# Causal attention in a vision transformer tower: element-major head stacks loaded in six transfers, class values by one bf16 product, tile loops written out

## The chip, the cores and the metric

The kernel runs on one core of one Trainium2 chip. The metric is the device time of one execution in microseconds (us), the median of three runs. Engine names follow the profile: PE is TensorE (matrix products), PEld its weight loads, DVE is VectorE, ACT is ScalarE, POOL is GpSimd, SP is SyncE, which here does nothing but issue DMA transfers.

## What is computed

The reference is a small tower on 8 images of 512 patches with 256 features, to which one class token per image is added in front. After a token projection four residual steps follow: a causal attention block with a feed-forward part, an FFN with blockwise 4-bit rounding, a state space block with a scan, and a last block with softmax attention plus a mixture of experts. The change is about the causal attention, with 16 heads of 16 features:

```python
def _attention(x, wq, bq, wk, bk, wv, bv, wo, bo):
    q = (x @ wq.T + bq).reshape(b, s, NH, D).transpose(0, 2, 1, 3)
    k = (x @ wk.T + bk).reshape(b, s, NH, D).transpose(0, 2, 1, 3)
    v = (x @ wv.T + bv).reshape(b, s, NH, D).transpose(0, 2, 1, 3)
    scores = jnp.einsum('bhqd,bhkd->bhqk', q, k) / jnp.sqrt(jnp.float32(D))
    causal = jnp.tril(jnp.ones((s, s), jnp.float32))
    att = jax.nn.relu(scores) * causal
    att = att / (jnp.sum(att, axis=-1, keepdims=True) + 1e-09)
    ctx = jnp.einsum('bhqk,bhkd->bhqd', att, v)
```

The weights are relu(score), not an exponential. The class token is key 0 and every query may look at it, so each patch query has one weight for the class key beside its 512 causal ones; the class query itself sees only its own key. The last block has the same 16 heads with a full softmax.

## The kernel before

Tokens lie in 33 tiles of 128: tile 0 holds the 8 class tokens, the other 32 are four tiles for each of 8 images ("batches"). The residual streams env.x, env.h and env.o stay in SBUF. The kernel is a row of passes, each with one program for each engine and semaphores between them; each pass frees its semaphores in `Area.clear` (L116) and closes with a barrier of all engines. The order of work in an engine's program is written out by hand. The passes, with their stretch of the trace in us: constants and tokens (0 to 180), `pass_qkv` (180 to 314), `pass_causal` (315 to 553), `pass_mlp` (554 to 860), `pass_fp4` (866 to 1188), `pass_ssm_in` (1190 to 1315), `pass_scan` (to 1383), `pass_moe` (to 1797), `pass_attend` (to 2276).

**Tile loops.** The generator `tiles` (L57) gives an engine its first three or five tiles written out, then a hardware loop of two tiles per turn, then a written-out tail. In the loop the values of waits and the addresses are computed in registers. `known(s)` is the tile number where it is a Python number and 9 in the loop.

**pass_qkv.** Per tile PE transposes the normalised tile (L495), forms q and k with 8 products (L505), v with 2 (L512), and 2 products of q with the class key, the scores against key 0 (L523, `class_scores`). DVE forms the statistics (L412, L415) and the normalised tile z (L421); POOL adds epsilon (`qkv_ve`, L406) and takes the power -1/2 (`qkv_rs`, L408). q and k in fp32 (`qkf`) are split in three bf16 parts each, whose sum is the fp32 number: ACT casts part 0 (L566), DVE subtracts it (`rest`, L622) and casts part 1 (L624), POOL subtracts again to part 2 (L588, `third`, three tiles behind the statistics). ACT takes relu of the class scores (`cls_s`, L572). SP writes per tile the parts (`qk_parts`, L463), v (L466) and the class scores (`cls_w`, L459) to scratch DRAM.

**pass_causal.** A product of two fp32 numbers is formed as six products of bf16 parts, all in one pass of PE: for one head of 16 elements the stack `qs` has 16 x 6 = 96 rows, with part PQ = (0,0,0,1,1,2) of q in the six rows of an element, and `ks` the part PK = (0,1,2,0,1,0) of k. `load_half` (L663) fills the stacks of 8 heads for one batch by 12 transfers of 16 rows each (L671), and loads the values (L672) and the class scores (L674). The 8 batches have 4 groups of 4 heads, in all 32 groups. A group has four key tiles: `scores` (L743, four heads, 512, 384, 256 and 128 query columns), relu and mask by ACT (L802, two heads, with POOL's mask of the diagonal block, L833) and by DVE (L863, the other two), then `values` (L757, fp32 weights by v, with a column of ones that sums them). Before a group's values `class_value` (L748) adds the class key's part: an fp32 product of `vbd`, 16 rows with the class value of each head in its own block, and `cls_w`, 16 rows with the class scores of the batch. `turn` (L769) transposes a finished group and DVE divides it.

At the start of the pass SP loads the class row of v, the constants `own`, `pick` and `causal` (L710 to L713), and then both halves of batch 0. PE forms `c8` (L728), spreads the class values over the heads (L732), DVE multiplies them by `own` into `vbd`, and only then do the scores begin. Later batches are loaded in a loop, each half when the values of the batch before it are done.

The stack part of `pass_attend` (`Heads.load`) fills its stacks in the same way, from the parts that `pass_moe` writes.

## Time and profile before

| | us |
|---|---|
| median of 3 runs | 2281.74 (2280.27 to 2282.27) |
| the profiled execution, its own time | 2278.18 |
| span of the trace in that execution | 2276.4 |
| PE busy in the span | 2098.8 (92%) |
| DVE / ACT / POOL busy | 1594.1 / 907.1 / 737.6 |

The span goes from the first to the last instruction in the trace; the execution's own time is 1.8 us longer. The median of the runs lies 3.6 us over the profiled execution. In the rows further down, a line of a timeline has start, duration, engine, line of the kernel, operation, output and inputs, shape, count, and in square brackets the time that the engine sat idle before it and what it waited for. A line of the view by windows has the stretch, its length, then busy time and instruction count of PE, PEld, DVE, ACT and POOL, the granted clock of PE (1.00 is full), the busy share of the DMA engines and GB/s. `SPq` is the issue of a DMA by SP.

### The profile page before, as it was taken

What the parts mean: (1) busy time and instruction counts of PE and PEld (TensorE: products, weight loads), DVE (VectorE), ACT (ScalarE), POOL (GpSimd) and SP (SyncE); (2) the same over time, 40 slices, a digit from 0 to 9 for tenths busy, and PEclk for the clock granted to TensorE, in tenths of its full rate; (3) what the DMA queues carried; (4) which work ended last, traced back from release to release, by engine and by line L of the source; (5) the groups of instructions that cost most, each with busy time, mean ns of one, the idle gap of its engine ahead of it and who ended that gap; (6) DMA issues with size and microseconds to landing.
All of it is one profiled execution on the core that took longest, in us unless ns stands there. A gap on an engine that the chain in (4) does not pass through costs nothing. (4 is left out here: it accounts for less than half of the span.)

```text
span 2276.4 us, 41030 instructions
## 1 busy us (share of the span) xinstructions
PE 2098.8 (92%) x11587; PEld 1337.9 (59%) x11587; DVE 1594.1 (70%) x4366; ACT 907.1 (40%) x2124; POOL 737.6 (32%) x1350
## 2 busy tenths in 40 slices
PE   7998969998999997999988958999999999999998
PEld 6886833333888885666663316888888523333332
DVE  3336846665677776888866856776777788888882
ACT  1114635553221223444433431222222157777777
POOL 3554525554333332333422101111111423333222
PEclk9998979998999999999998968999999779999999
DMA  4323665443000000000001010212214302232210
GB/s 135 114 90 86 152 181 144 138 133 108 1 0 0 0 0 14 1 0 0 0 24 37 9 31 20 48 37 47 46 38 125 89 10 76 81 95 78 76 44 20
DMA packets 215394, 132.43 MB, mean 58 GB/s; under 512 B 116675, under 2 KB 204309, under 8 KB 215317
## 3 DMA queue, kind: packets, MB, share of 16 engines
q1 hardware_dynamic: 215316, 131.50, 21.4%
q8 instruction: 36, 0.59, 0.1%
q14 instruction: 42, 0.34, 0.0%
HBM read 89.81 MB, written 41.25 MB: 58 GB/s over the span
## 5 line engine op out<-in xcount | busy, mean ns | idle before, releaser
L2547 DVE TENSOR_REDUCE attend_mx<-ps 128x1 f32<-128x512 f32 x512 | 320.9, 682 | 40.5 <-PE ps L2241 39.4
L2384 ACT ACTIVATE attend_w<-ps 128x512 f32<-128x512 f32 x512 | 280.6, 596 | 92.5 <-PE ps L2255 90.7
L1854 PE MATMUL ps<-keep_early,moe_zT 128*128 128x256 f32 x1056 | 243.4, 384 | 6.4 <-DVE keep_h L2009 4.4
L1854 PEld LDWEIGHTS ps<-keep_early,moe_zT 128*128 128x128 f32 x1056 | 196.5, 191 | 43.1 <-DVE keep_h L2009 18.6
L2241 PE MATMUL ps<-keep_x,keep_o 96*128 96x512 bf16 x512 | 209.8, 416 | 5.7 <-DVE attend_mx L2547 4.0
L2255 PE MATMUL ps<-keep_o,keep_x 99*128 99x512 bf16 x512 | 191.6, 384 | 2.7 <-ACT attend_w L2384 2.7
L2009 DVE SCALAR_TENSOR_TENSOR keep_h<-ps,moe_g,keep_h 128x256 f32 (+1 forms) x264 | 127.6, 483 | 61.5 <-PE ps L1854 53.2
L863 DVE SCALAR_TENSOR_TENSOR keep_early<-ps,causal_causal 128x512 f32<-128x512 f32 (+3 forms) x256 | 114.0, 486 | 80.2 <-PE ps L743 80.1
L2241 PEld LDWEIGHTS ps<-keep_x,keep_o 96*128 96x128 bf16 x512 | 50.3, 99 | 183.8 <-DVE attend_mx L2547 136.0
L833 POOL TENSOR_TENSOR keep_early<-keep_early,causal_causal 128x128 f32<-128x128 f32 x256 | 113.3, 458 | 128.7 <-ACT keep_early L802 127.7
L802 ACT ACTIVATE keep_early<-ps 128x512 f32<-128x512 f32 (+3 forms) x256 | 98.5, 435 | 126.3 <-PE ps L743 126.0
L2273 PE MATMUL ps<-attend_w,keep_early 128*17 128x512 f32 x1024 | 135.5, 598 | 0.0
L1072 PE MATMUL ps<-mlp_zT,keep_early 128*128 128x128 f32 x1056 | 127.7, 280 | 4.6 <-ACT mlp_zT L1114 4.6
L1072 PEld LDWEIGHTS ps<-mlp_zT,keep_early 128*128 128x128 f32 x1056 | 121.4, 193 | 12.3 <-ACT mlp_zT L1114 8.8
L276 PE MATMUL ps<-tok_W,tok_xin 128*128 128x256 f32 x512 | 122.5, 383 | 0.0
L1081 PE MATMUL ps<-keep_early,mlp_f 128*128 128x256 f32 x528 | 119.3, 379 | 0.0
L1081 PEld LDWEIGHTS ps<-keep_early,mlp_f 128*128 128x128 f32 x528 | 100.2, 190 | 13.6
L276 PEld LDWEIGHTS ps<-tok_W,tok_xin 128*128 128x128 f32 x512 | 96.0, 193 | 12.7 <-issue 0.7
L743 PE MATMUL ps<-causal_qs,causal_ks 96*128 96x256 bf16 (+3 forms) x512 | 93.8, 306 | 10.4 <-DMA causal_cls_w<-cls_w 9.9
L743 PEld LDWEIGHTS ps<-causal_qs,causal_ks 96*128 96x128 bf16 x512 | 37.5, 98 | 111.8 <-issue 57.8
L1274 PE MATMUL ps<-fp_wd,fp_hT 128*128 128x256 f32 x396 | 92.9, 385 | 2.8 <-ACT fp_hT L1306 2.8
L757 PE MATMUL ps<-keep_early,causal_v 128*17 128x512 f32 (+3 forms) x1024 | 95.2, 442 | 0.2 <-POOL keep_early L833 0.2
(332 smaller groups left out, 4064.2 us busy)
## 6 DMA issues: line engine op xcount, KB each, us to landing
tok_xin<-in_xk SPq DMA_DIRECT2D x64, 256.0 KB, 2.7
qk_parts<-qkv_parts SPq DMA_DIRECT2D x33, 384.0 KB, 3.2
qk_parts<-moe_parts SPq DMA_DIRECT2D x33, 384.0 KB, 3.2
causal_qs<-qk_parts SPq DMA_DIRECT2D x96, 128.0 KB, 2.7
causal_ks<-qk_parts SPq DMA_DIRECT2D x96, 128.0 KB, 2.7
keep_o<-qk_parts SPq DMA_DIRECT2D x96, 128.0 KB, 2.8
keep_x<-qk_parts SPq DMA_DIRECT2D x96, 128.0 KB, 2.8
v_all<-qkv_v SPq DMA_DIRECT2D x33, 136.0 KB, 3.1
```

The lines of the kernel that those rows point to most:

```text
L276: last = nc.tensor.matmul(ps[:, u, 0:D], xin[:, u, k, :], W[:, k // KD, k % KD, :], start=(k == 0), stop=(k == KT - 1))
L743: nc.tensor.matmul(ps[:, j, kt * P:S], ks[:, half, hh + j, kt * P:(kt + 1) * P], qs[:, half, hh + j, kt * P:S], start=True, stop=True).the ...
L863: nc.vector.scalar_tensor_tensor(w[:, j, kt % 2, 0:S - kt * P], ps[:, j, kt * P:S], 0.0, causal[:, 0:S - kt * P], ALU.max, ALU.mult).then_ ...
L1072: last = nc.tensor.matmul(ps[:, bank, m * P:(m + 1) * P], f1[:, k, f0:f0 + P], zT[:, k * P:(k + 1) * P], start=(k == 0), stop=(k == KD - 1))
L1081: last = nc.tensor.matmul(ps[:, F2, 0:D], f[:, m, :], f2[:, m, :], start=(m == 0), stop=(m == KF - 1))
L1854: last = nc.tensor.matmul(ps[:, E0 + pair % 2, e % 2 * D:(e % 2 + 1) * D], zT[:, u, k * P:(k + 1) * P], we[e][:, k, :], start=(k == 0), st ...
L2009: ins = nc.vector.scalar_tensor_tensor(env.h[:, s, :], ps[:, E0 + pair % 2, e % 2 * D:(e % 2 + 1) * D], g[:, u, 3, e:e + 1], env.h[:, s, : ...
L2241: nc.tensor.matmul(ps[:, MX + i % RING, :], qs[0:R, x.buf(0), h, t * P:(t + 1) * P], ks[0:R, x.buf(0), h, :], start=True, stop=True).then_ ...
L2255: nc.tensor.matmul(ps[:, SC + i % RING, :], ks[:, x.buf(2), HG * g + j, kt * P:(kt + 1) * P], qs[:, x.buf(2), HG * g + j, :], start=True, ...
L2273: last = nc.tensor.matmul(ps[2 * HD * j:2 * HD * j + HD + 1, CTX, :], v[:, buf, kt, (HG * g + j) * (HD + 1):(HG * g + j + 1) * (HD + 1)], ...
L2384: nc.scalar.activation(w[:, j, kt % 2, :], ps[:, SC + (HG * k + j) % RING, :], ACT.Exp)\
L2547: nc.vector.tensor_reduce(mx[:, t, k:k + 1], ps[:, MX + (TB * k + t) % RING, :], AX, ALU.max)\
```

## The change

1. **Order of head elements.** The host orders the columns of wq and wk (and their biases, the head mask, and the q and k part of W_qkv) by element first and head second. The scratch tensor is now (half, slot, row, tile, token) with six slots for each half of the heads; `part_of` writes q's parts in slots 0, 1, 2 and k's in slots 5, 4, 3. So `load_stacks` fills rows of three, two and one part by one transfer each for q and k: 6 transfers for a half, of 48, 32 and 16 rows, with the same bytes as the 12 before. `pass_attend` uses the same function.
2. **Class values in bf16.** The relu class scores are split in three bf16 parts as well: ACT writes the fp32 value and part 0, POOL forms parts 1 and 2 (`class_parts`, three instructions per tile, each waiting for the one before). The class values of tile 0 are split once by POOL (`class_value`), go by six small transfers to `diag_parts` and come back by 12 transfers as `vb`, 96 rows with zeros off the head's block. `class_value` on PE is then one bf16 product of 96 rows. The products with `pick`, the multiplication by `own`, and their loads are gone.
3. **Loads ahead.** Objects `Causal` and `Half` hold the buffers of half 0, the constants and the class stack; they are allocated around `pass_qkv`, in an area of their own that closes after `pass_causal`. SP loads the stacks of batch 0, half 0, behind tile 27 of `pass_qkv`, values and constants behind tile 28, the class stack behind tile 29. In the causal loop the stacks of the next batch wait for the scores, not for the values, and the class stack has two buffers. The class row of env.o is now multiplied after the last division.
4. **Loops.** `tiles` is a Python loop over all 33 tiles, in every pass but the token pass, which keeps the old form as `looped_tiles`. The batch loops of `pass_causal` are written out as well.

```diff
-def tiles(eng, peeled=3, tail=0):
+def tiles():
+    for s in range(NT):
+        yield s, s % 2, s // 2
+def looped_tiles(eng, peeled=3, tail=0):
-    with eng.Fori(0, (NT - peeled - tail) // 2) as i:
-        yield 2 * i + peeled, 1, i + peeled // 2
-        yield 2 * i + peeled + 1, 0, i + peeled // 2 + 1
...
+SLOTS = 6
+RUNS = ((0, 3), (3, 2), (5, 1))
...
+def part_of(parts, u, c):
+    return parts[:, u, :, c:SLOTS - c:SLOTS - 1 - 2 * c, :].rearrange("p m q t -> p q m t")
+def load_stacks(sp, io, m, b, qs, ks, sem):
+    for at, n in RUNS:
+        rows = slice(0, 2 * HD * n, 2) if at == 0 else slice(2 * HD * (at - 3) + 1, 2 * HD * (at - 3 + n), 2)
+        for dst, slot in ((qs, 0), (ks, SLOTS - n)):
+            src = io["qk_parts"][m, slot:slot + n, :, bass.ds(1 + TB * b, TB), :].rearrange("c (d h) n t -> (c d) h (n t)", d=HD)
+            sp.dma_start(dst[rows, :, :], src).then_inc(sem, 16)
+STACKS = 16 * 2 * len(RUNS)
...
-                sp.wait_ge(s_cls, s)
+                sp.wait_ge(s_clsp, s)
                 sp.sem_inc(s_took, 1)
-                sp.dma_start(io["cls_w"][:, s - 1, :], cls_s[:, u, :]).then_inc(s_cout[u], 16)
-            for s, u, n in tiles(sp, 5):
+                sp.dma_start(io["cls_parts"][:, :, s - 1, :].rearrange("c h t -> h c t"), cls_p[:, s % 4, :, :])\
+                    .then_inc(s_cout[s % 4], 16)
+            def class_value_rows():
...
+                for c in range(3):
+                    for half in range(2):
+                        sp.dma_start(io["diag_parts"][c, 0:1, half, :].rearrange("b (h x) -> b h x", h=HALF)[:, :, 0:HD + 1],
+                                     v0p[:, c, half * HALF * (HD + 1):(half + 1) * HALF * (HD + 1)]
+                                     .rearrange("b (h d) -> b h d", d=HD + 1)).then_inc(s_diag, 16)
+            for s, u, n in tiles():
                 sp.wait_ge(s_p2, s + 1)
-                sp.dma_start(io["qk_parts"][:, :, :, s, :].rearrange("c m p t -> p (c m) t"),
-                             parts[:, u, :, :].rearrange("p c (m t) -> p (c m) t", t=P)).then_inc(s_out[u], 16)
+                sp.dma_start(io["qk_parts"][:, :, :, s, :].rearrange("m j p t -> p (m j) t"),
+                             parts[:, u, :, :, :].rearrange("p m j t -> p (m j) t")).then_inc(s_out[u], 16)
                 sp.wait_ge(s_va, s + 1)
                 sp.dma_start(io["v_all"][s], v[:, u, :, :].rearrange("p h d -> p (h d)")).then_inc(s_vout[u], 16)
-                if known(s) >= 1:
-                    class_out(s, u)
+                if known(s) >= 2:
+                    class_out(s - 1, 1 - u)
+                if isinstance(s, int) and s == 4:
+                    class_value_rows()
+                if isinstance(s, int) and s == NT - LATE:
+                    for w in range(2):
+                        sp.wait_ge(s_out[w], 16 * 3)
+                        sp.wait_ge(s_vout[w], 16 * 3)
+                    for w in range(4):
+                        sp.wait_ge(s_cout[w], 16)
+                    ahead.first.load_stacks(sp, io, 0)
+                if isinstance(s, int) and s == NT - LATE + 1:
+                    sp.wait_ge(s_diag, 16 * 6)
+                    ahead.first.load_values(sp, io, 0)
+                    sp.wait_ge(s_zero, 1)
+                    ahead.load_constants(sp, io)
+                if s == NT - LATE + 2:
+                    ahead.load_class(sp, io, 0)
...
-                nc.scalar.copy(parts[:, u, 0, :], qkf[:, u, :]).then_inc(s_p0, 1)
+                nc.scalar.copy(part_of(parts, u, 0), by_block(qkf[:, u, :])).then_inc(s_p0, 1)
...
-                nc.scalar.activation(cls_s[:, u, :], ps[0:NH, 6 + u, 0:P], ACT.Relu).then_inc(s_cls, 1)
-            for s, u, n in tiles(act, 5):
+                past(act, s_cout[s % 4], 16 * ((s - 1) // 4))
+                nc.scalar.activation(cls_s[:, s % 4, :], ps[0:NH, 6 + u, 0:P], ACT.Relu)
+                nc.scalar.activation(cls_p[:, s % 4, 0, :], ps[0:NH, 6 + u, 0:P], ACT.Relu).then_inc(s_cls, 1)
...
-                nc.gpsimd.tensor_tensor(parts[:, u, 2, :], rest[:, u, :], parts[:, u, 1, :], ALU.subtract)\
+                nc.gpsimd.tensor_tensor(part_of(parts, u, 2), by_block(rest[:, u, :]), part_of(parts, u, 1), ALU.subtract)\
...
+            def class_parts(s):
+                u = s % 4
+                ch = Chain(pool, c_cls, 2 * (s - 1))
+                pool.wait_ge(s_cls, s)
+                pool.sem_inc(s_took, 1)
+                ch.link(nc.gpsimd.tensor_tensor(cls_r[:, :], cls_s[:, u, :], cls_p[:, u, 0, :], ALU.subtract))
+                pool.sem_inc(s_took, 1)
+                ch.link(nc.gpsimd.tensor_copy(cls_p[:, u, 1, :], cls_r[:, :]))
+                pool.sem_inc(s_took, 1)
+                nc.gpsimd.tensor_tensor(cls_p[:, u, 2, :], cls_r[:, :], cls_p[:, u, 1, :], ALU.subtract).then_inc(s_clsp, 1)
...
+            for s, u, n in tiles():
                 ln.on_pool(pool, s, u)
                 if known(s) >= 3:
                     third(s - 3, 1 - u)
+                if known(s) == 3:
+                    class_value()
+                if known(s) >= 5:
+                    class_parts(s - 4)
+            class_parts(NT - 4)
             for s in range(NT - 3, NT):
                 third(s, s % 2)
+                class_parts(s)
...
-    for c in range(len(PQ)):
-        for m, dst, part in ((half, qs, PQ[c]), (2 + half, ks, PK[c])):
-            src = io["qk_parts"][part, m, :, bass.ds(1 + TB * b, TB), :].rearrange("(h d) n t -> d h (n t)", d=HD)
-            sp.dma_start(dst[c:HD * len(PQ):len(PQ), :, :], src).then_inc(sem, 16)
...
+    def load_constants(self, sp, io):
+        sp.dma_start(self.causal[:, :], io["causal"]).then_inc(self.s_const, 16)
+        for at, n in RUNS:
+            for c in range(n):
+                for half in range(2):
+                    row = NH * (at + c) + HALF * half
+                    sp.dma_start(self.vb[row:row + HALF, half, :],
+                                 io["diag_parts"][n - 1 - c, 0, half, 0:HALF * HALF * 2 * HD].rearrange("(h x) -> h x", h=HALF))\
+                        .then_inc(self.s_const, 16)
+    def load_class(self, sp, io, b):
+        for at, n in RUNS:
+            sp.dma_start(self.cls[NH * at:NH * (at + n), b % 2, :],
+                         io["cls_parts"][0:n, :, TB * b:TB * (b + 1), :].rearrange("c h n t -> (c h) (n t)"))\
+                .then_inc(self.s_cls[b % 2], 16)
...
-            for half in range(2):
-                load_half(sp, io, 0, half, qs[:, half], ks[:, half], v[:, half], cls_w[:, half, :], s_load[half])
+            halves[1].load_stacks(sp, io, 0)
+            halves[1].load_values(sp, io, 0)
+            sp.dma_start(v0[:, :], io["v_all"][0, 0:B, :]).then_inc(s_w, 16)
             env.ahead["mlp"].start(sp)
-            with sp.Fori(1, B) as b:
+            for b in range(1, B):
+                if b >= 2:
+                    sp.wait_ge(s_pv, STEPS * (b - 2) + TB * (NG - 1) + 1)
+                ahead.load_class(sp, io, b)
                 for half in range(2):
+                    sp.wait_ge(s_sc[HG - 1], STEPS * (b - 1) + STEPS // 2 * (half + 1))
+                    halves[half].load_stacks(sp, io, b)
                     sp.wait_ge(s_pv, STEPS * (b - 1) + STEPS // 2 * (half + 1))
-                    load_half(sp, io, b, half, qs[:, half], ks[:, half], v[:, half], cls_w[:, half, :], s_load[half])
+                    halves[half].load_values(sp, io, b)
...
-            nc.tensor.matmul(ps[0:NH, 7, 0:NH * (HD + 1)], pick[:, :], v0[:, :], start=True, stop=True).then_inc(s_vps, 1)
-            pe.wait_ge(s_vbd, 1)
+            pe.wait_ge(s_const, CONSTS)
...
-                    pe.wait_ge(s_load[half], 16 * LOADS * (b + 1))
+                    pe.wait_ge(s_stacks[half], STACKS * (b + 1))
...
             def class_value(b, g):
+                if g % 2 == 0:
+                    pe.wait_ge(s_values[g // 2], 16 * (b + 1))
+                if g == 0:
+                    pe.wait_ge(ahead.s_cls[b % 2], 16 * len(RUNS) * (b // 2 + 1))
                 past(pe, s_ctxs, NG * b + g - 1)
-                nc.tensor.matmul(ps[:, 4 + g % 2, :], vbd[:, HG * g:HG * (g + 1), :].rearrange("h a d -> h (a d)"),
+                at = 2 * HD * HG * (g % 2)
+                nc.tensor.matmul(ps[:, 4 + g % 2, :], vb[:, g // 2, at:at + 2 * HD * HG], ahead.cls[:, b % 2, :],
...
-            dve.wait_ge(s_vps, 1)
-            nc.vector.tensor_tensor(vbd[:, :, 0:HD + 1],
-                                    ps[0:NH, 7, 0:NH * (HD + 1)].rearrange("p (h d) -> p h d", d=HD + 1),
-                                    own[:, :, :], ALU.mult).then_inc(s_vbd, 1)
+            dve.wait_ge(s_const, CONSTS)
...
+            if step is pass_qkv:
+                env.causal = Causal(nc)
+                with env.causal.area.ctx:
+                    env.causal.reserve()
+                    pass_qkv(nc, env, io)
+                    pass_causal(nc, env, io)
```

**Places where the order of instructions moves.** POOL, from one tile to the next in the steady part of `pass_qkv`, before (`qkv_ve` and `qkv_rs` are the statistics, `qkv_parts` is `third`):

```order
L588 TENSOR_TENSOR qkv_parts<-qkv_rest,qkv_parts 128x512
L403 REGISTER_ALU
L405 REGISTER_ALU
L406 TENSOR_TENSOR qkv_ve<-qkv_mv,keep_eps 128x1
L408 TENSOR_TENSOR qkv_rs<-qkv_ve,keep_mhalf 128x1
L588 TENSOR_TENSOR qkv_parts<-qkv_rest,qkv_parts 128x512
L63 REGISTER_ALU
L63 COMPARE_AND_BRANCH
```

and after:

```order
L659 TENSOR_TENSOR qkv_parts<-qkv_rest,qkv_parts 128x2x2x128
L667 TENSOR_TENSOR qkv_cls_r<-qkv_cls_s,qkv_cls_p 16x128
L669 CAST qkv_cls_p<-qkv_cls_r 16x128
L671 TENSOR_TENSOR qkv_cls_p<-qkv_cls_r,qkv_cls_p 16x128
L415 TENSOR_TENSOR qkv_ve<-qkv_mv,keep_eps 128x1
L417 TENSOR_TENSOR qkv_rs<-qkv_ve,keep_mhalf 128x1
L659 TENSOR_TENSOR qkv_parts<-qkv_rest,qkv_parts 128x2x2x128
```

Behind each `third` there are now three instructions on the 16 rows of class scores; the register instructions and the branch are gone.

SP, from the last tile of `pass_qkv` into `pass_causal`, before:

```order
L459 DMA cls_w<-qkv_cls_s 16x128
L63 REGISTER_ALU
L63 COMPARE_AND_BRANCH
L434 UNCONDITIONAL_BRANCH
L708 UNCONDITIONAL_BRANCH
L710 DMA causal_v<-v_all 128x272
L711 DMA causal_own<-in_own 16x272
L712 DMA causal_pick<-in_row_pick 128x16
L713 DMA causal_causal<-in_causal 128x512
L671 DMA causal_qs<-qk_parts 16x8x512
L671 DMA causal_ks<-qk_parts 16x8x512
```

and after, the place behind tiles 27 and 28 (`first_qs` and `first_ks` are the stacks of half 0):

```order
L516 DMA qk_parts<-qkv_parts 128x12x128
L519 DMA v_all<-qkv_v 128x272
L501 DMA cls_parts<-qkv_cls_p 16x3x128
L458 DMA first_qs<-qk_parts 48x8x512
L458 DMA first_ks<-qk_parts 48x8x512
L458 DMA first_qs<-qk_parts 32x8x512
L458 DMA first_ks<-qk_parts 32x8x512
L458 DMA first_qs<-qk_parts 16x8x512
L458 DMA first_ks<-qk_parts 16x8x512
L516 DMA qk_parts<-qkv_parts 128x12x128
L519 DMA v_all<-qkv_v 128x272
```

The 12 transfers of 16 rows at the head of the causal pass have become six, and stand between the output of tile 27 and that of tile 28. Between tiles 28 and 29 SP issues 14 more, between 29 and 30 another three.

PE, start of `pass_causal`, before:

```order
L728 MATMUL ps<-keep_head_mask,causal_prod 8x16 x2
L732 MATMUL ps<-causal_v,causal_pick 16x272
L743 MATMUL ps<-causal_qs,causal_ks 128x512 x4
L748 MATMUL ps<-causal_cls_w,causal_vbd 128x512
L743 MATMUL ps<-causal_qs,causal_ks 128x384 x4
L757 MATMUL ps<-keep_early,causal_v 17x512 x4
```

and after:

```order
L862 MATMUL ps<-keep_head_mask,causal_prod 8x16 x2
L875 MATMUL ps<-first_qs,first_ks 128x512 x4
L885 MATMUL ps<-first_cls,first_vb 128x512
L875 MATMUL ps<-first_qs,first_ks 128x384 x4
L894 MATMUL ps<-keep_early,first_v 17x512 x4
```

The product with `causal_pick` is gone, and the class product takes its operands from the new stacks.

## Rows read from the trace of the kernel before

**Rows 1.** Busy time of each engine in the whole span, with its share

```profile
PE 2098.8 (92%) x11587; PEld 1337.9 (59%) x11587; DVE 1594.1 (70%) x4366; ACT 907.1 (40%) x2124; POOL 737.6 (32%) x1350
```

**Rows 2.** Windows: qkv, causal, fp4, ssm; engines, PEclk, DMA share, GB/s

```profile
198.66:305.00 106.34, 106.34 (x777) 87.98 (x777) 87.11 (x201) 66.59 (x208) 62.02 (x86) 1.00 0.68 153
328.00:552.00 224.00, 221.07 (x1728) 79.11 (x1728) 143.25 (x442) 115.66 (x288) 113.28 (x256) 0.98 0.48 137
912.00:1140.00 228.00, 212.22 (x908) 154.52 (x908) 195.16 (x504) 96.59 (x203) 87.07 (x150) 1.00 0.00 0
1197.00:1254.00 57.00, 48.00 (x121) 18.45 (x122) 40.12 (x103) 22.25 (x46) 11.98 (x32) 0.86 0.09 25
```

**Rows 3.** Timeline, PE, from the last qkv product to the first scores

```profile
306.12 0.60 PE L523 MATMUL ps<-qkv_qkf,keep_kbd 128*16 128x128 f32 x4 [0.73 <-ACT qkv_cls_s L572]
315.63 0.28 PE L728 MATMUL ps<-keep_head_mask,causal_prod 128*8 128x16 f32 x4 [8.91 <-DVEq L842]
328.00 1.86 PE L743 MATMUL ps<-causal_qs,causal_ks 96*128 96x512 bf16 x4 [8.36 <-DMA causal_cls_w<-cls_w]
```

**Rows 4.** Timeline, SP, the first stack transfer of the causal pass

```profile
316.38 0.77 SPq L671 DMA_DIRECT2D causal_qs<-qk_parts  x1
```

**Rows 5.** Timeline, PE, score and class products in a later causal group

```profile
337.77 1.04 PE L743 MATMUL ps<-causal_qs,causal_ks 96*128 96x512 bf16 x4
...
339.07 1.12 PE L748 MATMUL ps<-causal_cls_w,causal_vbd 16*128 16x512 f32 x2
340.13 0.82 PE L743 MATMUL ps<-causal_qs,causal_ks 96*128 96x384 bf16 x4
```

**Rows 6.** Timeline, POOL, one steady tile of the qkv pass

```profile
266.83 0.19 POOL L406 TENSOR_TENSOR qkv_ve<-qkv_mv,keep_eps 128x1 f32<-128x1 f32 x1 [0.86 <-DVE qkv_mv L415]
267.10 1.02 POOL L408 TENSOR_TENSOR qkv_rs<-qkv_ve,keep_mhalf 128x1 f32<-128x1 f32 x1
268.16 1.16 POOL L588 TENSOR_TENSOR qkv_parts<-qkv_rest,qkv_parts 128x512 bf16<-128x512 f32 x1
...
270.45 0.55 POOL L408 TENSOR_TENSOR qkv_rs<-qkv_ve,keep_mhalf 128x1 f32<-128x1 f32 x1
```

**Rows 7.** DVE in the qkv pass: L421 over 33 tiles; timeline of one split

```profile
L421 DVE TENSOR_SCALAR qkv_z<-keep_x,qkv_mv,qkv_rs x33: 399/1092/1237, 184.1 to 296.8; 128x256 f32 x26, 128x256 f32<-128x256 f32 x7
...
266.93 0.69 DVE L622 TENSOR_TENSOR qkv_rest<-qkv_qkf,qkv_parts 128x512 f32<-128x512 f32 x1 [0.26 <-ACT qkv_parts L566]
...
267.65 0.43 DVE L624 CAST qkv_parts<-qkv_rest 128x512 bf16<-128x512 f32 x1
```

**Rows 8.** POOL elsewhere: page section 5, then two lines of the timeline

```profile
L833 POOL TENSOR_TENSOR keep_early<-keep_early,causal_causal 128x128 f32<-128x128 f32 x256 | 113.3, 458 | 128.7 <-ACT keep_early L802 127.7
...
1824.88 1.15 POOL L2415 TENSOR_TENSOR attend_nrest<-keep_early,attend_nparts 16x512 f32<-16x512 f32 x1
1826.20 0.61 POOL L2417 CAST attend_nparts<-attend_nrest 16x512 bf16<-16x512 f32 x1 [0.17 <-POOL attend_nrest L2415]
```

**Rows 9.** Page section 6; timeline: SP's output of tile 29, ACT's cast, small issues

```profile
qk_parts<-qkv_parts SPq DMA_DIRECT2D x33, 384.0 KB, 3.2
...
297.94 0.38 SPq L463 DMA_DIRECT2D qk_parts<-qkv_parts  x1
...
301.80 0.62 ACT L566 CAST qkv_parts<-qkv_qkf 128x512 bf16<-128x512 f32 x1
...
1801.11 2.02 SPq L2184 DMA_DIRECT2D diag_parts<-attend_v0p  x6
```

**Rows 10.** PE's loop branches (ns, min/median/max), PE's waits for loads, 330 to 552

```profile
L63 PEldq COMPARE_BRANCH  x71: 76/208/234, 45.0 to 1782.0; - x71
...
PE ps L743 <- DMA causal_cls_w<-cls_w: 1.5, 4, 0.6
```

**Rows 11.** Timeline, PE, the same 16 products in the ssm pass twice

```profile
1250.37 8.83 PE L1529 MATMUL ps<-ssm_zT,keep_early 128*128 128x512 f32 x16 [0.46 <-ACT ssm_zT L1572]
...
1266.83 7.13 PE L1529 MATMUL ps<-ssm_zT,keep_early 128*128 128x512 f32 x16 [0.46 <-ACT ssm_zT L1572]
```

228 lines of the change are left out of this document (133 added, 95 removed).

## The prediction

> **What bounds the kernel now.** First the page's busy times: PE works 92% of the span [rows 1], so what is not on PE or does not make PE wait costs nothing. Then the windows, pass by pass [rows 2]. In the qkv pass PE is busy for 106.34 of 106.34 us at full clock. A tile there is 26 matrix products, so 777 records are 29.9 tiles and the period is 106.34/29.9 = 3.56 us; POOL works 62.02 us of it, 2.07 a tile. In the causal pass PE is busy 221.07 of 224.00 us: 32 groups in the 216 us after the first, slow one, some 6.74 us each, and DVE, ACT and POOL have a third to a half of the time free. So in both passes the sum of PE's products sets the time, and anything else counts only where it makes PE wait. The third view is PE's timeline between the two passes [rows 3]: its last qkv product ends at 306.72, the first scores start at 328.00. That is 21.3 us with hardly any work on PE, and the change reaches into it.
>
> **The class product.** In a group, the four bf16 score products of 512 columns take 1.04 us from the start of the first to the end of the last, so one holds PE for 0.26 us at most; I use 0.25. The fp32 class product starts at 339.07 and the next scores at 340.13: it holds PE for 1.06 us [rows 5]. The new one is a single bf16 product of 96 rows and 512 columns, the same form as a score product. Gain 1.06 - 0.25 = 0.81, times 32 groups = 25.9. The other side of the bound is that the next engine is then late: ACT, DVE and POOL have 3.6, 4.5 and 3.5 us of work per group (115.66, 143.25 and 113.28 over 32 [rows 2]) against the new period of 5.9, so PE stays the bound, but its pauses for relu and mask may grow. I take **-25**, bounds -26 and -20.
>
> **The handover.** Before, the first stack transfer leaves at 316.38 [rows 4], behind the loads of v0, own, pick and the mask; then come the other eleven of the half, values and class scores, and PE gets the last at 328.00 [rows 3]. After, half 0, values, `vb` and the class stack have long landed when the pass starts; PE needs only the product at 315.63 and its 0.28 us, so scores may start at 315.95. That is 12.0 us less. Against it stands what SP now does within the qkv pass. Behind tile 27 it issues six transfers at about 0.7 us (0.77 for the first stack transfer [rows 4]) = 4.2 us, behind tile 28 one for values, one for the mask and 12 small ones of 0.34 (2.02 us for six [rows 9]), 5.2 us, behind tile 29 three = 1.2 us: 10.6 us in three tiles of 3.56, where SP already issues three outputs a tile. Tile 28's output is late by 4 and tile 29's by some 6 us. ACT's cast of tile 31 at 301.80 may only begin when tile 29's output, issued at 297.94 [rows 9], has landed; an output takes 3.2 us to land [rows 9], so the cast has 301.80 - 297.94 - 3.2 = 0.7 us of slack, and behind it stand the class chain and the end of the pass. The pass can lose from 0 (SP catches up, the last tiles wait for nothing) to 10 us (all of it). I take +4, so the handover is **-8**, bounds -12 and -2.
>
> **The rate of the qkv pass.** This is the term that I am least sure of. POOL gets three instructions more per tile. No row has their shape, 16 rows by 128. A subtraction of 128 columns takes 0.458 elsewhere; I use 0.43 for 16 rows. 16 by 512 takes 1.15 for the subtraction, and 0.61 for the cast, from which I set the cast of 128 columns at 0.29, with 0.17 between linked instructions [rows 8]. POOL's chain in a tile is then 0.19 + 0.08 + 0.55 + 0.05 + 1.16 [rows 6] and (0.43 + 0.17 + 0.29 + 0.17 + 0.43 + 0.17) with 0.05 between: 3.74 us without any disturbance, already over 3.56. There is disturbance. `qkv_rs` takes 0.55 in one tile and 1.02 in the next [rows 6]; the long one, 267.10 to 268.12, ends with DVE's cast (267.65 + 0.43 = 268.08 [rows 7]). The normalisation takes DVE 0.40 at best and 1.09 at the median [rows 7]: it starts when `qkv_rs` is done, as does POOL's `third`. With one such stretch of 0.4 a tile POOL's period is 4.15 us. PE waits then for z. Over the 28 tiles with class parts in the steady part that is 28 x (4.15 - 3.56) = **+16.5**. Bounds: 0, if the three instructions are shorter than their nearest rows and fall in the 0.86 us gaps that POOL has, and +29 from the rival below. `class_value`, once, is four instructions of 272 columns in one row; DVE's value of tile 2 waits for it and PE's v product behind that. I take **+2**, bounds 0 and 3.
>
> **The rest.** Written-out loops take away PE's branch, 208 ns at the median, 71 times in five passes [rows 10]. In the qkv pass they sit under gap-free PE, and there they cost nothing today. The mlp, fp4 and causal passes have 15 + 14 + 7 of them: 36 x 0.208 = 7.5 at most; other engines wait there as well, and so I take half, **-4**, bounds -7.5 and 0. The loads of the later batches made PE wait 1.5 us four times in all [rows 10]; with half the transfers and an earlier start I take **-1.5**. The one more barrier of all engines at the end of the causal pass and the class row's product before it: **+0.9**, bounds 0.5 and 2. In the attention pass, stacks with half as many transfers load beside gap-free PE: 0. ACT's second activation on 16 rows fits in its 1.3 us of free time a tile: 0.
>
> **Sum.** -25 - 8 + 16.5 + 2 - 4 - 1.5 + 0.9 = -19.1. The profiled execution took 2278.18 by its own clock, its span being 2276.4; it would take 2259.1. The median of the runs is 3.6 higher than that execution, 2281.74, and the forecast for it is 2281.74 - 19.1 = **2263**.
>
> **Rivals.** (B) POOL's added work is hidden: the small subtractions on 16 rows are cheaper than 128-row ones, and PE keeps 3.56 us. For it speaks that POOL has 1.49 us a tile free and the three might be 1.1; against it that the chain of waits, not the busy time, counts. The sum is then -19.1 - 16.5 = -35.6: 2246.
>
> (C) DVE and POOL exclude each other in the qkv pass. The rows show one waiting for the other in `qkv_rs` and in the normalisation [rows 6, 7]. If nothing of either can overlap, a tile costs POOL's own 0.19 + 0.55 + 1.16 + 1.15 = 3.05 and DVE's 0.40 + 0.69 + 0.43 = 1.52 [rows 7], 4.57 us, one 4.6. That is 28 x 1.04 = +29 in place of +16.5: 2275. The Trainium skill, "SBUF — State Buffer", section "Who interferes with whom", states such a rule: the two engines share one pair of ports, and whoever issues first holds it for the whole instruction. By that rule the sum would be C's, and the stretched rows agree with it; against its full price speaks that `third` takes its 1.16 us in rows where DVE works beside it.
>
> (D) slower than before. The qkv pass loses PE's closeness. The granted clock was 1.00 in the gap-free qkv window and in the fp4 window with 212.22 of 228.00 us busy, but 0.86 in the ssm window, where PE worked 48.00 of 57.00 us in pieces [rows 2]; 16 products with some of the lower clock in them took 8.83 instead of 7.13 us [rows 11]. With C's period PE would pause for a microsecond in every tile too. A mean of 0.86 between the levels of 2.4 and 1.2 GHz is 28% of the time at the lower one, where a tile takes 7.1 us and not 4.6. With x such tiles of 28, 7.1x is 28% of 7.1x + 4.6 (28 - x), x = 5.6, and the loss 5.6 x 2.5 = 14 us more than C: 2289. It needs C's period, and it ends slower than before as soon as five tiles run at the lower level: 5 x 2.5 = 12 over 2275.
>
> (E) The change does not do what it says: the class product costs as much as before because its new operands (a stack over two buffers, three transfers a batch) come late. Then -25 is about -5, 2283.
>
> **Chances.** A, as summed, 0.50 (its own range 2252 to 2272); B 0.20; C 0.15; D 0.11; E 0.04. The likeliest is A, so 2263. The range goes from 2242 (B with a handover at its best) to 2280 (C with the pass's end late) and leaves out D, E and the tails, 2 in 10. A measurement of this kernel can tell about 0.2%, 4.6 us, from no change, so "same" is 2277.2 to 2286.3. Faster: A, B and three quarters of C, 0.81. Same: the rest of C, E and the edge of D, 0.09. Slower: 0.10.
>
> **What the profile after would show.** The class product's row 0.25 us and the causal groups some 5.9 us apart: term one. PE's first scores near 316 plus what the qkv pass grew: term two, and in SP's queue the outputs of tiles 28 and 29 late with ACT's cast waiting for a DMA. PE in the qkv window busy for 3.56 of 4.15 us a tile, idle before the transposes, with POOL as releaser through z, tells A from B (no idle) and C (4.6). Granted clock below 0.95 there speaks for D. Wrong I would be, above all, if POOL's small instructions cost other than their neighbours in the rows, or if the last four tiles of the pass wait in a row for SP.

## The result, and the profile after

| | before | after |
|---|---|---|
| median, us | 2281.28 (4 runs) | 2264.03 (4 runs, 2262.70 to 2264.74) |
| ratio to before | | 0.9924, 95% interval 0.9907 to 0.9941 |
| the profiled execution, its own time | 2278.18 | 2264.74 |
| span of its trace | 2276.4 | 2263.0 |

The change made the kernel 17 us faster; 2263 had been predicted. The two profiled executions differ by 13.4 us only, because that of before was 3 us under its median and that of after 0.7 us over. The ledger below is made between the two traces and must therefore come to 13.4. A trace is one execution: how long a pass takes differs between traces of the same code, the causal pass most of all (see e9).

The page of after, first lines:

```profile
span 2263.0 us, 36794 instructions
PE 2067.7 (91%) x11553; PEld 1333.7 (59%) x11553; DVE 1593.1 (70%) x4364; ACT 908.7 (40%) x2156; POOL 783.0 (35%) x1451
```

PE has 31 us less to do than in [rows 1], and the kernel is only 13 to 17 us shorter: part of what PE was spared came back as waiting. POOL has 45 us more. The view by windows of after, columns as in [rows 2], shows where. The first line is the steady qkv pass, the second the first 43.5 us of causal groups, the third a later stretch of them:

```profile
198.66:300.00 101.34, 87.94 (x630) 71.13 (x629) 76.07 (x169) 59.27 (x196) 83.46 (x145) 1.00 0.50 131
...
346.50:390.00 43.50, 40.26 (x310) 14.29 (x308) 26.92 (x82) 21.22 (x53) 20.72 (x47) 0.86 0.91 194
...
430.00:470.00 40.00, 40.00 (x364) 14.86 (x357) 30.02 (x95) 23.76 (x61) 24.12 (x55) 1.00 0.87 168
```

In the qkv pass, 630 records of 26 a tile are 24.2 tiles: 4.18 us a tile, against 3.56, with PE idle for 0.55 us in each. The granted clock stays at its full level all the same.

**The ledger.** Starts and ends are those of PE's instructions: when the first of its line starts, when the last does.

| stretch | before | after | difference |
|---|---|---|---|
| start of the qkv transposes | 184.6 | 185.6 | +1.0 |
| first to last transposes of the qkv pass | 113.9 | 132.3 | +18.4 |
| last transposes to the first causal scores | 29.5 | 28.6 | -0.9 |
| first scores to the last turn | 223.7 | 199.1 | -24.6 |
| last turn to the first `up` products of the feed-forward pass | 17.8 | 18.4 | +0.6 |
| feed-forward pass, first to last of these | 291.9 | 288.3 | -3.6 |
| to the end of the 4-bit FFN (1187.9 / 1178.1) | 326.5 | 325.8 | -0.7 |
| to the end of the state space products (1321.5 / 1309.9) | 133.6 | 131.8 | -1.8 |
| to the end of the mixture products (1794.5 / 1779.4) | 473.0 | 469.5 | -3.5 |
| rest, to the end of the span | 481.9 | 483.6 | +1.7 |

The head of the causal pass in PE's timeline of after, to be set beside [rows 3]; the first line is the small product at its start, the second the first scores:

```profile
346.29 0.27 PE L862 MATMUL ps<-keep_head_mask,causal_prod 128*8 128x16 f32 x4 [10.86 <-DVEq L979]
346.50 1.89 PE L875 MATMUL ps<-first_qs,first_ks 96*128 96x512 bf16 x4
```

### The profile page after: what moved, and what is told of

Same layout as the page of the kernel before. It is cut to its first block and busy times, and to the rows that moved or that the text cites. A ratio compares the mean times of both kernels' runs of the same rounds, so it can differ in the third digit from the quotient of the medians.

```text
span 2263.0 us, 36794 instructions
## 1 busy us (share of the span) xinstructions
PE 2067.7 (91%) x11553; PEld 1333.7 (59%) x11553; DVE 1593.1 (70%) x4364; ACT 908.7 (40%) x2156; POOL 783.0 (35%) x1451
## 5 line engine op out<-in xcount | busy, mean ns | idle before, releaser
L2143 DVE SCALAR_TENSOR_TENSOR keep_h<-ps,moe_g,keep_h 128x256 f32<-128x256 f32 x264 | 127.6, 483 | 61.3 <-PE ps L1988 53.8
L993 DVE SCALAR_TENSOR_TENSOR keep_early<-ps,first_causal 128x512 f32<-128x512 f32 (+3 forms) x256 | 114.0, 486 | 52.6 <-PE ps L875 48.4
L971 POOL TENSOR_TENSOR keep_early<-keep_early,first_causal 128x128 f32<-128x128 f32 x256 | 113.3, 458 | 89.3 <-ACT keep_early L939 88.3
L415 POOL TENSOR_TENSOR moe_ve<-moe_mv,keep_eps 128x1 f32<-128x1 f32 x33 | 6.3, 192 | 266.4 <-DVE moe_mv L424 266.4
L2071 POOL TENSOR_TENSOR moe_parts<-moe_rest,moe_parts 128x512 bf16<-128x512 f32 x33 | 38.2, 1156 | 142.5 <-DVE moe_parts L2123 142.5
L1392 PE MATMUL ps<-fp_wg,fp_zT 128*128 128x352 f32 x264 | 86.1, 470 | 1.4 <-ACT fp_zT L1466 1.4
```

Source lines behind the costliest of these rows:

```text
L971: nc.gpsimd.tensor_tensor(w[:, j, kt % 2, 0:P], w[:, j, kt % 2, 0:P], causal[:, 0:P], ALU.mult).then_inc(s_p[j], 1)
L993: nc.vector.scalar_tensor_tensor(w[:, j, kt % 2, 0:S - kt * P], ps[:, j, kt * P:S], 0.0, causal[:, 0:S - kt * P], ALU.max, ALU.mult).then_ ...
L2143: ins = nc.vector.scalar_tensor_tensor(env.h[:, s, :], ps[:, E0 + pair % 2, e % 2 * D:(e % 2 + 1) * D], g[:, u, 3, e:e + 1], env.h[:, s, : ...
```

## Experiments

All start from the changed kernel; 2264.03 is the time to compare with. Each time is a median of 4 or 5 runs with its range. Two kernels of this table have to be 3 us apart or more before a difference means much: the ranges of single runs are up to 9 us wide. They were measured in three sets (e1 to e4, e5 to e8, e9 to e12); the kernel before ran again in each and took 2281.28, 2281.76 and 2281.09, so the sets can be compared. The changed kernel has no runs in these sets.

| | us | range from | to |
|---|---|---|---|
| e1, class parts left out on POOL | 2246.87 | 2243.56 | 2249.59 |
| e2, early loads at the causal start | 2262.18 | 2260.63 | 2265.91 |
| e3, loops put back in four passes | 2271.82 | 2270.53 | 2275.20 |
| e4, twelve transfers | 2267.54 | 2264.90 | 2271.50 |
| e5, early loads spread | 2252.04 | 2249.83 | 2256.30 |
| e6, class parts staged | 2248.72 | 2245.14 | 2251.04 |
| e7, part 1 on ACT | 2252.87 | 2249.76 | 2256.28 |
| e8, e5 and e7 | 2242.62 | 2241.82 | 2245.41 |
| e9, class product twice | 2265.66 | 2263.62 | 2268.93 |
| e10, e5 and e6 | 2239.58 | 2235.82 | 2243.63 |
| e11, e10 with the weights later | 2242.94 | 2238.66 | 2247.30 |
| e12, e11 with part 1 on ACT, lagged | 2242.49 | 2238.00 | 2246.98 |

### What sets the rate of the qkv pass: e1, e6, e7

```diff
             def class_parts(s):
-                ch = Chain(pool, c_cls, 2 * (s - 1))
                 pool.wait_ge(s_cls, s)
...
-                nc.gpsimd.tensor_tensor(cls_p[:, u, 2, :], cls_r[:, :], cls_p[:, u, 1, :], ALU.subtract).then_inc(s_clsp, 1)
+                pool.sem_inc(s_clsp, 1)
```

> The changed kernel, with POOL's three instructions per tile on the class scores left out: parts 1 and 2 of the class scores stay zero, so the class scores lose their low bits and nothing else is left out. In the changed kernel the 24.2 tiles between 198.66 and 300 us took 4.18 us each, PE busy 87.94 of 101.34 us. Theory (POOL's chain sets the rate of the qkv pass): with the three gone the tile falls back to 3.56 us, PE is busy without gaps, and the kernel gains 28 x 0.62 = 17 us: 2247 against 2264. Rival (the strided part writes of ACT, DVE and POOL, or the second ACT activation, slow the tile): it stays at about 4.2 us and the time stays near 2264. The wait of ACT for the outputs of tiles 28 and 29 should stay in either case.

Measured: 2246.87, 17.2 us less. The window of e1 over the same stretch:

```profile
198.66:300.00 101.34, 98.26 (x718) 80.84 (x717) 83.81 (x194) 67.30 (x224) 56.76 (x87) 1.00 0.58 149
```

That is 27.6 tiles; PE is idle for 3.1 us in all, in two waits for z of at most 1.6 us each (in the view of waits), and for the rest a tile takes its 3.56 us without a gap. The strided part writes, the second ACT activation and the bf16 class output are all still in this kernel, so in the steady tiles they cost nothing, and POOL's three instructions are the cause. One of the two waits, 1.51 us at 201.2, follows POOL's four instructions on the class values: that is the split, once. Between the traces the stretch from first to last transposes is 14.6 us shorter in e1 (117.6 for 132.2); most of the rest of the 17.2 is a causal stretch of 194.1 and not 199.1 us, of which more under e9.

The second question was what of those instructions it is. In e6 they are the same, but none waits for the one before:

```diff
+            def staged(s):
+                if 1 <= s - 4 < NT:
+                    class_rest(s - 4)
+                if True and 1 <= s - 5 < NT:
+                    class_second(s - 5)
+                if 1 <= s - 6 < NT:
+                    class_third(s - 6)
```

> The changed kernel with POOL's three class instructions of a tile taken from three different tiles (rest of tile s-4, part 1 of tile s-5, part 2 of tile s-6), so that none waits for the one before; same instructions, same engine, class output three tiles behind. Theory (part of POOL's 4.18 us are the pauses of 0.17 to 0.24 between linked instructions): 0.5 us a tile go, 3.7 us, 13 us gained, 2251. Rival (POOL and DVE exclude each other, so that the time goes into stretched instructions instead): POOL's busy time per tile rises from 3.45 us and the period stays over 4.0: 2260 to 2264. Removing work from POOL altogether gave 17 us.

Measured: 2248.72, 15.3 us less. POOL's groups of instructions over 198.66 to 300 us, after (columns: count | busy, mean ns of one | idle before, what it waited for):

```profile
L659 POOL TENSOR_TENSOR qkv_parts<-qkv_rest,qkv_parts 128x512 bf16<-128x512 f32 x25 | 28.9, 1155 | 0.9 <-DVE qkv_parts L730 0.9
L669 POOL CAST qkv_cls_p<-qkv_cls_r 16x128 bf16<-16x128 f32 x23 | 14.3, 622 | 3.9 <-POOL qkv_cls_r L667 3.9
L417 POOL TENSOR_TENSOR qkv_rs<-qkv_ve,keep_mhalf 128x1 f32<-128x1 f32 x25 | 14.1, 565 | 2.0
L671 POOL TENSOR_TENSOR qkv_cls_p<-qkv_cls_r,qkv_cls_p 16x128 bf16<-16x128 f32 x23 | 11.7, 511 | 4.1 <-POOL qkv_cls_p L669 4.1
L667 POOL TENSOR_TENSOR qkv_cls_r<-qkv_cls_s,qkv_cls_p 16x128 f32<-16x128 f32 x23 | 10.8, 470 | 0.0
L415 POOL TENSOR_TENSOR qkv_ve<-qkv_mv,keep_eps 128x1 f32<-128x1 f32 x25 | 5.6, 225 | 6.9 <-POOL qkv_cls_p L671 5.9 <-DVE qkv_mv L424 0.8 <-POOL qkv_v0p L686 0.2
```

and the same of e6:

```profile
L662 POOL TENSOR_TENSOR qkv_parts<-qkv_rest,qkv_parts 128x512 bf16<-128x512 f32 x28 | 32.3, 1152 | 6.2 <-DVE qkv_parts L743 6.0
L417 POOL TENSOR_TENSOR qkv_rs<-qkv_ve,keep_mhalf 128x1 f32<-128x1 f32 x28 | 20.3, 726 | 2.2
L415 POOL TENSOR_TENSOR qkv_ve<-qkv_mv,keep_eps 128x1 f32<-128x1 f32 x28 | 13.1, 470 | 1.5 <-DVE qkv_mv L424 1.1 <-POOL qkv_v0p L700 0.2
L668 POOL TENSOR_TENSOR qkv_cls_r<-qkv_cls_s,qkv_cls_p 16x128 f32<-16x128 f32 x26 | 12.2, 468 | 0.0
L678 POOL TENSOR_TENSOR qkv_cls_p<-qkv_cls_r,qkv_cls_p 16x128 bf16<-16x128 f32 x24 | 11.6, 482 | 0.0
L673 POOL CAST qkv_cls_p<-qkv_cls_r 16x128 bf16<-16x128 f32 x25 | 7.0, 279 | 0.0
```

In after, POOL sits idle for 3.9, 4.1 and 5.9 us before linked instructions, 0.60 us a tile, and its cast takes 622 ns at the mean. In e6 these pauses are gone and the cast takes 279 ns, but `qkv_ve` and `qkv_rs` are stretched in turn, 225 to 470 and 565 to 726. POOL's busy time for one tile is nearly the same, 83.46 us over 24.2 tiles = 3.45 us in after and 91.72 over 27.0 = 3.40 in e6; what fell is its idle time, from 0.74 to 0.36 us. So it is the pauses, and not the work, that staging takes away. The prediction's price of the cast (0.29) was right for a cast alone; the stretch is what happens beside DVE. A pair from the timeline of after, one tile with and one without it:

```profile
305.77 0.28 POOL L669 CAST qkv_cls_p<-qkv_cls_r 16x128 bf16<-16x128 f32 x1 [0.17 <-POOL qkv_cls_r L667]
305.80 0.80 DVE L728 TENSOR_TENSOR qkv_rest<-qkv_qkf,qkv_parts 128x512 f32<-128x512 f32 x1
...
309.67 0.84 POOL L669 CAST qkv_cls_p<-qkv_cls_r 16x128 bf16<-16x128 f32 x1 [0.17 <-POOL qkv_cls_r L667]
309.69 0.67 DVE L728 TENSOR_TENSOR qkv_rest<-qkv_qkf,qkv_parts 128x512 f32<-128x512 f32 x1
```

At 305 POOL's cast is first and DVE's subtraction is 0.13 us longer than its 0.67; at 309, with 0.02 us between the starts, the cast takes 0.56 us longer and ends 0.15 behind DVE. One of the two is held while the other runs. The Trainium skill, "SBUF — State Buffer", section "Who interferes with whom", states this as a rule, for a DVE instruction with both inputs in SBUF too; these rows agree that one of them is held. They do not bear out its second half, that whoever issues first keeps the ports, as far as the start of a row tells who issued first: POOL's row starts first in both pairs, and it keeps its 0.28 us in one and is held in the other. What does not follow is that all their times add. The rival that added them came to 4.57 us a tile; after measured 4.18. In e6, with the same instructions on the same engines, the window has 701 records, which is 3.76 us a tile. That blocked time falls in part into waits that would have been there anyway is my reading of this; no run isolates it.

In e7 the cast goes to ACT:

```diff
+            def second(s):
+                act.wait_ge(s_r, s)
+                nc.scalar.copy(cls_p[:, s % CB, 1, :], cls_r[:, s % 4, :]).then_inc(s_c1, 1)
```

> As the kernel before in this set, but part 1 of the class scores is cast by ACT instead of POOL. Theory: POOL's work in a tile is 0.19 + 0.55 + 1.16 + 0.47 + 0.42 = 2.8 us plus a stretch of 0.4 and small pauses, under PE's 3.56, ACT has 2.8 of 3.56: the tile is bound by PE again, 2247 as with no class parts at all. Rival (POOL and DVE exclude each other in full: 2.8 + 1.52 = 4.3): the period stays over 3.9 us, 2258 or more.

Measured: 2252.87, 678 records in the window, 3.89 us a tile: worse than all three on POOL, and my theory of a PE-bound tile was wrong. The trace names the cause, POOL waiting for ACT before the second subtraction, in the timeline of e7:

```profile
232.47 0.82 POOL L686 TENSOR_TENSOR qkv_cls_p<-qkv_cls_r,qkv_cls_p 16x128 bf16<-16x128 f32 x1 [0.33 <-ACT qkv_cls_p L643]
...
237.39 0.73 POOL L686 TENSOR_TENSOR qkv_cls_p<-qkv_cls_r,qkv_cls_p 16x128 bf16<-16x128 f32 x1 [1.60 <-ACT qkv_cls_p L643]
```

In the same window these waits come to 14.0 us, 0.54 a tile.

### What the early loads cost: e2, e5

The end of the qkv pass in the timeline of after, SP and ACT:

```profile
311.84 0.66 SPq L458 DMA_DIRECT2D first_qs<-qk_parts  x1
...
315.80 0.59 SPq L516 DMA_DIRECT2D qk_parts<-qkv_parts  x1
...
316.44 4.30 SPq L519 DMA_DIRECT2D v_all<-qkv_v  x1
...
320.87 0.35 SPq L501 DMA_DIRECT2D cls_parts<-qkv_cls_p  x1
...
322.29 4.04 SPq L805 DMA_DIRECT2D first_vb<-diag_parts  x12
326.37 0.39 SPq L516 DMA_DIRECT2D qk_parts<-qkv_parts  x1
...
323.44 0.62 ACT L637 CAST qkv_parts<-qkv_qkf 128x512 bf16<-128x512 f32 x1 [6.54 <-DMA qk_parts<-qkv_parts]
...
329.70 0.62 ACT L637 CAST qkv_parts<-qkv_qkf 128x512 bf16<-128x512 f32 x1 [4.04 <-DMA qk_parts<-qkv_parts]
...
333.34 0.62 ACT L637 CAST qkv_parts<-qkv_qkf 128x512 bf16<-128x512 f32 x1 [1.98 <-DMA qk_parts<-qkv_parts]
```

ACT's three casts wait 12.6 us in all for outputs, and with them the end of the pass. The three waits have different causes. The first, of 6.54 us, is for the output of tile 28. Its parts were ready at 313.30, when POOL's `third` of that tile ends; SP, still issuing stack transfers, sends it at 315.80. And then it takes 7.5 us to land, where such an output otherwise takes 3.2, in the view of transfers over 311.8 to 317 us:

```profile
qk_parts<-qkv_parts SPq DMA_DIRECT2D x1, 384.0 KB, 7.5
```

So 2.5 us of it are SP's issues and 4.3 us the slow landing behind the six stack transfers. The second wait, 4.04 us, is for the output of tile 29, whose parts were ready at 317.51 and which SP sends at 326.37: the issue of v, otherwise 0.66 to 0.82 us, had held it for 4.30 us and the twelve of `vb` for 4.04. This output lands in 3.2 us again. The third, 1.98 us, is for tile 30, sent 2.1 us late behind the class stack. The blocked issue of v alone is not the cause: in e4 (below) the same issue takes 0.86 us behind twelve stack transfers, and ACT's casts wait 14.2 us.

```diff
-                    ahead.first.load_stacks(sp, io, 0)
...
+            ahead.first.load_stacks(sp, io, 0)
+            ahead.first.load_values(sp, io, 0)
+            ahead.load_constants(sp, io)
+            ahead.load_class(sp, io, 0)
             halves[1].load_stacks(sp, io, 0)
```

> The changed kernel with the early loads of half 0, constants and class stack moved from tiles 27 to 29 of the qkv pass to the start of the causal pass, in the same order. In the changed kernel the last transposes of the qkv pass are followed by 28.6 us to the first scores, in the kernel before by 29.5 us; ACT's casts waited 6.54, 4.04 and 1.98 us for outputs. Theory (the early loads cost in the end of the qkv pass what they save at the head of the causal pass): the three waits of ACT go, the pass ends about 11 us earlier, the first scores then wait for 6 + 1 + 13 + 3 transfers, some 13 us after the pass starts; the total moves by less than 3 us either way. Rival (the early loads are a gain of about 8 us, as the prediction had it): this kernel is 8 us slower, 2272.

Measured: 2262.18, 1.9 us less, within the 3 us of the first theory and far from 2272. The last class scores of the pass start at 326.6 and not 335.0, and PE then waits for the loads (total, times and longest, in us):

```profile
PE ps L866 <- DMA first_vb<-diag_parts: 13.4, 1, 13.4
```

As it stands in the changed kernel, loading ahead brings nothing in the whole. The trace shows that the balance is not made in one place: in e2 the causal scores start 5.2 us later than in after, at 351.7, and the causal stretch is 6.4 us shorter, 192.7 us, because there PE does not wait for the stacks of batch 1 (see e9). e5 keeps the early loads, and gives each tile from 8 to 24 one or two of the transfers:

```diff
+                if 8 <= s < 14:
+                    next(loads)
+                if s == 14:
+                    ahead.first.load_values(sp, io, 0)
...
+                if 15 <= s < 22:
+                    next(consts)
...
+                if 22 <= s < 25:
+                    next(classes)
```

> The changed kernel with the same early loads, but spread over the qkv pass: one stack transfer behind each of tiles 8 to 13, values at 14, mask at 15, two vb transfers behind each of 16 to 21, class stack behind 22 to 24. Theory (the end of the qkv pass grows because SP issues some 23 transfers in three tiles and the outputs of tiles 28 to 30 leave late): ACT's waits of 6.54, 4.04 and 1.98 us go, the pass ends about 11 us earlier and the first scores keep their early start: 2253. Rival (it is the bytes in the queues, not SP's time at the end, or the transfers disturb the outputs wherever they are): the tiles 8 to 24 get slower and the gain is under 4 us, 2260 or more.

Measured: 2252.04, 12.0 us less. The steady window has 632 records, so that the tiles are no slower with the transfers among them, and the last class scores start at 327.4, the first causal ones at 339.2 instead of 346.5. That is 7.3 of the 12.0 us, less than the 11 of the theory; the causal stretch is 5.6 us shorter as well, 193.5 us. The view of waits of e5, ACT from 200 to 360 us (in total, times, longest), has no long one; the same view of after has 17.4, 7, 6.5:

```profile
ACT qkv_parts L644 <- DMA qk_parts<-qkv_parts: 7.7, 7, 2.2
```

How much of the longer end of the pass the loads are worth can be read from the time between the last transposes and the product at the head of the causal pass: 17.1 us before, 28.4 in after, 20.8 in e2 and e5 alike. So the lump of loads costs 7.6 us there. The other 3.7 us have another cause: with POOL's instructions staged as well (e10, below) it is 16.7 us, no more than before. They are POOL's linked instructions on the class scores of the last tiles, at the very end of the pass.

### Loops and transfers: e3, e4

```diff
-            for s, u, n in tiles():
+            for s, u, n in looped_tiles(pe, 5):
```

> The changed kernel with the hardware loops of the kernel before put back in the feed-forward, 4-bit FFN, state space and mixture passes (qkv and causal stay written out). Between the two traces these passes got shorter by 3.6, 0.7, 2.0 and 3.0 us. Theory (all of that is the loops): this kernel is slower by 9 us, 2273, each pass by its own number. The prediction's value was 4 us in all, nothing of it in the mixture pass: 2268. Rival (the shorter passes come from somewhere else, as the place at which the granted clock falls, and the loops cost nothing): 2264.

Measured: 2271.82, 7.8 us more, near the 9 of the theory and twice the prediction's 4. Pass by pass the theory does not hold. From the first to the last product with a tile of the pass, in us:

| | before | after | e3 |
|---|---|---|---|
| feed-forward | 302.7 | 299.1 | 305.0 |
| 4-bit FFN | 310.7 | 310.0 | 310.0 |
| state space | 147.3 | 145.5 | 147.1 |
| mixture | 412.0 | 408.9 | 413.3 |

The loops are worth nothing in the 4-bit FFN, and in the feed-forward and mixture passes more than between before and after. Together they are 11.9 us in this trace; its causal stretch is 4.8 us shorter than that of after, which hides part of them. The mixture pass has no term in the prediction. In the view by windows, 380 us of it in before, after and e3, in this order:

```profile
1400.00:1780.00 380.00, 376.47 (x2125) 324.96 (x2126) 267.97 (x865) 86.02 (x278) 57.43 (x90) 1.00 0.26 61
```

```profile
1390.00:1770.00 380.00, 380.00 (x2154) 328.80 (x2153) 266.67 (x868) 86.47 (x279) 60.55 (x91) 1.00 0.29 64
```

```profile
1391.00:1771.00 380.00, 374.96 (x2118) 323.43 (x2119) 266.58 (x863) 86.00 (x278) 57.41 (x90) 1.00 0.28 61
```

PE had 3.5 us without work before, none after, and 5.0 with the loops back. These windows do not start at the same place: a wait of 4.37 us, which all three kernels have, ends at 1401.5 in before and at 1392.7 in e3 and so lies in their windows for 1.5 and 1.7 us, while that of after ends ahead of its window, at 1389.4. What the loops leave idle is 2.0 us before, none after and 3.3 us in e3, in 26 short pauses of 0.06 to 0.32 us. It is less than the pass got longer (3.1 and 4.4 us); the rest shows as longer busy time of PE.

```diff
     for at, n in RUNS:
-        rows = slice(0, 2 * HD * n, 2) if at == 0 else slice(2 * HD * (at - 3) + 1, 2 * HD * (at - 3 + n), 2)
+        for c in range(n):
+            base, odd = (c, 0) if at == 0 else (at - 3 + c, 1)
+            rows = slice(2 * HD * base + odd, 2 * HD * (base + 1), 2)
```

> The changed kernel with each stack filled by 12 transfers of 16 rows again, 128 KB each, in both attentions; everything else as changed. Theory (loads lie beside work of PE in both attentions, and only SP's issue time at the end of the qkv pass counts): six more issues of 0.6 us behind tile 27, 3.6 us more of ACT's wait, and PE's waits for later batches grow by about 1.5 us: 4 to 5 us slower, 2269. Rival 1 (the number of transfers is all in the shade): 2264. Rival 2 (the 384 KB transfers are slower to land, 4.5 and 5.7 us against 2.8, and cost the last attention 1.8 us): faster by up to 2 us, seen in the attention pass alone.

Measured: 2267.54, 3.5 us more, with a range that touches that of the changed kernel (2264.90 against 2264.74). The direction and size are those of the first theory, and the trace shows both of its terms, though 3.5 us is little against the ranges: from the last transposes to the first scores it is 30.2 us and not 28.6, with 14.2 us of ACT's waits for 12.6, and PE waits 5.5 us for the stacks of batch 1 and not 3.2, the causal stretch being 200.7 us for 199.1. The last attention is 468.5 us from its first scores to its last values and so no worse for the shorter transfers. Half the number of transfers is at best a small gain, and the 384 KB ones harm nothing.

### Does PE bound the causal pass, and the first batches: e9, e11

```diff
+                for again in range(2):
+                    nc.tensor.matmul(ps[:, 4 + g % 2, :], vb[:, g // 2, at:at + 2 * HD * HG], ahead.cls[:, b % 2, :],
+                                     start=(again == 0), stop=False, skip_group_check=True)
```

> The changed kernel with each of the 32 bf16 class products issued twice into the same bank, so that the class value counts double. Theory (PE bounds the causal pass, and one such product holds it for 0.24 us): 32 x 0.24 = 7.7 us slower than the changed kernel, 2272, and groups 6.05 us apart instead of 5.82. Rival (with the shorter product another engine bounds the pass): under 2 us.

One group of after in PE's timeline:

```profile
401.76 1.04 PE L875 MATMUL ps<-first_qs,first_ks 96*128 96x512 bf16 x4
...
403.07 0.39 PE L885 MATMUL ps<-first_cls,first_vb 96*128 96x512 bf16 x1
403.30 0.81 PE L875 MATMUL ps<-first_qs,first_ks 96*128 96x384 bf16 x4
...
407.67 1.04 PE L875 MATMUL ps<-first_qs,first_ks 96*128 96x512 bf16 x4
```

and of e9:

```profile
403.61 1.04 PE L875 MATMUL ps<-first_qs,first_ks 96*128 96x512 bf16 x4
...
404.92 0.61 PE L886 MATMUL ps<-first_cls,first_vb 96*128 96x512 bf16 x2
405.37 0.81 PE L875 MATMUL ps<-first_qs,first_ks 96*128 96x384 bf16 x4
...
409.73 1.04 PE L875 MATMUL ps<-causal_qs,causal_ks 96*128 96x512 bf16 x4
```

The product holds PE for 0.23 us (403.07 to 403.30), against 1.06 in [rows 5]. The groups are 5.91 us apart in after and 6.12 in e9: the added product is in the period in full, so PE is the bound. (The added product is 0.21 us, less than the 0.24 expected.) Yet the median of e9 is only 1.6 us higher, and the whole causal stretch 199.9 us against 199.1, where 32 x 0.21 = 6.7 was due. The difference is in the first 43.5 us. There PE waits for nothing in e9 and has 354 records at a granted clock of 0.93; in after it has 310 at 0.86, with this wait in the timeline:

```profile
374.99 1.54 PE L875 MATMUL ps<-first_qs,first_ks 96*128 96x512 bf16 x4 [3.24 <-DMA first_ks<-qk_parts]
```

It is the start of batch 1, and the products behind the wait run at the lower clock for some 7 us, to 382.4 (four scores of 512 columns take 1.54 instead of 1.04 us). The two groups around it are 9.93 and 8.34 us long in place of 5.90, which makes 6.5 us in all. So a shorter product made PE reach batch 1 before its stacks, and part of the gain went back. How much differs from one execution to the next. With the same causal code e3 waited 1.5 us, kept the full clock behind the wait and needed 194.3 us for the stretch; e1 waited 0.9 us and needed 194.1, e5 0.5 and 193.5, e6 1.9 and 196.0. Against these, the 199.9 us of e9 are about 6 us more, near the 6.7 that were due. The two traces are so close because the one pays for its product and the other for its wait; that the medians are so close for the same reason is likely, but not shown.

SP issues the next pass's weights, 5.33 us for one of the five, ahead of batch 1. The hold by itself makes little: the first stack transfer of batch 1 leaves at 359.95, 13.5 us behind the first scores. In e11 it leaves 13.0 us behind them, where SP waits for nothing but the scores that free the buffer. What is late is the landing. e11 puts the weights behind batch 1:

```diff
-            env.ahead["mlp"].start(sp)
             for b in range(1, B):
...
+                if b == 1:
+                    env.ahead["mlp"].start(sp)
```

> As e10, with the five loads of the next pass's weights moved from the start of the causal pass behind the loads of batch 1. In the changed kernel one of those issues held SP for 5.33 us, PE waited 3.2 us for the stacks of batch 1, and the granted clock was 0.86 in the first 43 us of the pass. Theory (SP's blocked queue makes the first loads late): PE's wait goes, 3 us faster than e10. Rival (the stacks of batch 1 are late because their buffers come free late): within 1 us of e10, the wait stays.

Measured: 2242.94 against 2239.58 of e10, ranges overlapping, no gain. The wait did not go; it stands one batch later, in the timeline of e11:

```profile
374.53 1.04 PE L921 MATMUL ps<-first_qs,first_ks 96*128 96x512 bf16 x4 [2.83 <-DMA first_ks<-qk_parts]
```

The first scores of e11 start at 322.8, so this is the start of batch 2, the one behind the weights now; batch 1 has no wait. The wait follows the weights' transfers: the values of batch 1, issued last of its loads, take 11.5 us to land in after and 6.6 in e11, and those of batch 2 in e11 10.3. My rival, that the buffers come free late, was wrong as well: they come free at the same point in e11, and the wait at batch 1 is gone. That it is the bytes of the weights (two transfers of 1 MB) in the queue is the reading that is left; no run leaves them out.

### A version that is better than both: e8, e10, e12

> Loads spread over the qkv pass and part 1 cast by ACT, together. If the two costs are separate terms of the sum, the gains add: 17 + 11 us below the changed kernel, 2236. If with the tile at 3.56 us the spread transfers become the bound (three outputs and one or two loads of SP in 3.56 us), the tile stays over 3.7 us and the sum falls short: 2240 or more.

Measured: 2242.62. Short of the 2236 by 6.6 us; e7, which is half of it, had fallen short by 5.9. The window of e8 has 659 records, 4.00 us a tile. That is over the 3.7 named above, but the trace gives another reason than SP's transfers: POOL waits 16.7 us for ACT's cast between 198 and 305 us, as in e7.

> Loads spread over the qkv pass and POOL's class instructions staged over three tiles, all on POOL. Single gains against the changed kernel were 12 and 15.3 us. If they add: 2237. If the tail of the pass was partly the same time in both (with staging alone the class scores ended 18.4 us behind the last transposes, against 17.1 unstaged, and the spread version 9.2): 2240.

Measured: 2239.58, ratio to before 0.9819, 95% interval 0.9805 to 0.9833. The gains of e5 and e6, 12.0 and 15.3, nearly add: 24.5 us below the changed kernel, 41.7 below before. The end of the qkv pass is as short as before (16.7 us from the last transposes to the head of the causal pass).

> As e11, with part 1 cast by ACT and part 2 taken by POOL one tile later still (tile s-7). In the version with ACT and no such lag POOL waited up to 1.6 us for ACT's cast and the tile took about 3.85 us. Theory (the hand-over between the engines was the cost): POOL no longer waits for ACT, the tile falls to 3.56 us against 3.76 with all on POOL: 4 to 5 us faster than e11. Rival (DVE's and POOL's mutual exclusion holds the tile at 3.8): within 1 us of e11.

Measured: 2242.49, no better than e11. The tile did fall to nearly PE's own time, 714 records in the window, 3.69 us, and the first scores start 2.5 us earlier than in e11, at 320.3; but PE then waits 3.9 us for stacks of the causal pass. The gain is given back at the next load, as in the step before.

## Why the prediction came out right, step by step

The sum was -19.1, the medians moved by -17.3. The mechanism that it named as likeliest is what happened. Two of its terms were off by 7.1 and 5.6 us, in opposite directions. Between the two traces, from which the ledger is made, the difference is only -13.4, 5.7 less than the sum.

- **The class product, -25.** Groups 5.91 us apart against the 6.74 that the prediction read: 0.83 x 32 = -26.6. Right, and PE is still the bound (e9). Before, 6.74 was the median; with pauses in some groups the mean behind the first group was 6.84, and these pauses are gone as well.
- **Loads of later batches, -1.5.** Wrong in sign in the trace of after. Before they cost 1.5 us; now PE arrives earlier and waits 3.24 us at batch 1, with a lower clock behind it, 6.5 us in all. This and the class product together came to -24.6 in the trace, and to about -29 in executions where the wait was short (e1, e3).
- **The rate of the qkv pass, +16.5, and the split of class values, +2.** Measured +18.4 between first and last transposes, 4.18 us a tile for 4.15, and -17.2 when the per-tile work is taken out (e1; -14.6 in that stretch of its trace). The estimate stood on two halves that both held: linked pauses count (e6 gets 15 us back by taking them away, 12.6 of it in this stretch), and one stretched instruction a tile. It was not right in the detail of which one: not `qkv_rs` but POOL's cast, 622 ns at the mean.
- **The handover, -8.** The step that failed. -0.9 was measured. The head of the causal pass did shrink from 12.4 us (315.6 to 328.0) to 0.2 (346.29 to 346.50), but the end of the qkv pass grew by 11.3 us instead of the +4 that I took, beyond the upper bound of 10. Of these, 7.6 are the early loads (e2, e5) and 3.7 the linked class instructions of the last tiles (e5 against e10), for which the sum had no term. For the loads I had counted SP's issue times alone, from single issues, with every output landing in 3.2 us. The output of tile 28 was 2.5 us late where I had 4, but took 7.5 us to land behind the six stack transfers; that of tile 29 was 8.9 us late where I had 6, because one issue took 4.30 us.
- **Loops, -4.** Undersized. -9.6 between the traces in the four rows of the ledger, 7.8 in e3 (11.9 in the four passes of its trace). The sum had terms for the feed-forward, 4-bit FFN and causal passes and none for the mixture pass, which had 14 of the branches and became 3.1 us shorter; in the 4-bit FFN, with 14 as well, the loops were worth nothing.
- **Barrier, +0.9.** +0.6 measured.
- Rival B (POOL's work hidden) fell with the 4.18 us a tile and with e1. Rival C (all of DVE's and POOL's time adds) fell by its size, 4.18 for 4.57 us, though its mechanism is in the rows. Rival D (a lower clock in the qkv pass) fell: 1.00 in the steady tiles. Only behind the waits at the end of the pass did it fall, to 0.73 from 318 to 346 us. Rival E (the class product stays dear) fell with its row, 0.23 us.

So the closeness of 2263 to 2264.0 owes something to luck. The handover was 7 us too good, the loops nearly 6 us too small, and the rest of the agreement lies in which executions were traced: the medians differ by 3.9 us more than the traces.

## What to carry to other kernels

Work that is moved ahead is not free where it is put: give a DMA queue its extra transfers one or two per step over many steps, never in a lump before outputs that others wait for; the same loads cost 7.6 us at the end of the pass in three tiles and nothing in seventeen. They cost in two ways, in the time of the queue's issuer and in the landing of what is issued behind them. On an engine that is near the bound, linked short instructions on one small tile cost their pauses as much as their work: take them from different steps, so that no one waits for its neighbour. When a pass gets shorter, look at once at what is loaded behind it, since that load is now on the path.

## What the runs showed of the hardware that I had not expected

- One DMA issue of SP took 4.30 us in the qkv pass, where the other 32 of its line take 0.66 to 0.82 us, and one of 128 KB in the causal pass 5.33 us, where the kernel before takes 1.03 us for it. Both stand behind several large transfers in a row (six stack transfers and an output; three of the weights, two of them 1 MB). Behind twelve stack transfers of 128 KB (e4) the issue took 0.86 us; what makes the difference stays open. Twelve small ones in a row took 4.04 us, 0.34 each.
- An output of 384 KB took 7.5 us to land behind six stack transfers and 3.2 us otherwise.
- A POOL cast of 16x128 takes 0.28 us alone and 0.84 beside a DVE subtraction with both inputs in SBUF that starts at the same time; the other way round the subtraction grows from 0.67 to 0.80.
- PE with a pause of half a microsecond in each 4.18 us, 87% busy, kept the full granted clock through 101 us, while a single pause of 3.24 us in the causal pass was followed by some 7 us at the lower one, and one of 1.5 us in the same place (e3) by none.
